# A graph layer with residual and normalisation: more pairs turned by VectorE, normalisation one pair later, a part of it on VectorE, loads issued from two queues

## The reference

```python
# x: 50000 x 512 float32; src, dst: 62500 edges, among them one loop per node; W_l, W_r: 512 x 512
msg  = x[src]
agg  = segment_sum(msg, dst, num_segments=n)
deg  = segment_sum(ones, dst, num_segments=n)
mean = agg / maximum(deg, 1.0)[:, None]
h    = mean @ W_l + b + x @ W_r
out  = layernorm(x + h * sigmoid(h), axis=-1)      # (u - mean(u)) / sqrt(var(u) + 1e-5)
```

## Time and profile before

| | |
|---|---|
| median of three executions | 1533.49 us (1531.86 to 1535.54) |
| the profiled execution | 1532.49 us, of which 1530.7 us are its span |
| PE busy | 1498.7 us (98% of the span) |
| PE weight loads | 1240.8 us (81%) |
| DVE busy | 1320.3 us (86%) |
| ACT busy | 1180.0 us (77%) |
| POOL busy | 1025.4 us (67%) |
| moved by DMA | 397.68 MB, mean 260 GB/s |

### The profile page before, as it was taken

The page is one execution under the profiler, slowest core; times in us unless marked ns, Lnnn a source line. Parts: engine busy times, 40 slices in busy tenths (PEclk is TensorE's granted clock), DMA queues, the critical chain, the costliest instruction groups (busy, mean ns, idle before and its releaser), DMA issues.

```text
span 1530.7 us, 23969 instructions
## 1 busy us (share of the span) xinstructions
PE 1498.7 (98%) x7198; PEld 1240.8 (81%) x7198; DVE 1320.3 (86%) x2090; ACT 1180.0 (77%) x1603; POOL 1025.4 (67%) x1089
## 2 busy tenths in 40 slices
PE   8999999999999999999999999999999999999996
PEld 6887778888888778888888888888888888888885
DVE  7988999999997878888888888888888888887886
ACT  5454333333334889999999999999999999999997
POOL 6446566666662766766767767667777777777774
PEclk9999999999999999999999999999999999999998
DMA  6476688989987789999989999999999999999996
GB/s 208 156 223 189 203 253 266 267 260 264 268 267 214 205 251 287 287 276 278 276 263 298 274 283 282 277 280 270 277 285 270 279 275 288 289 274 270 291 271 199
DMA packets 299349, 397.68 MB, mean 260 GB/s; under 512 B 43036, under 2 KB 145206, under 8 KB 299221
## 3 DMA queue, kind: packets, MB, share of 16 engines
q1 hardware_dynamic: 252277, 321.93, 70.5%
q0 software_dynamic: 46944, 74.22, 18.0%
HBM read 333.87 MB, written 139.67 MB: 309 GB/s over the span
## 4 chain that ended last, share of the span: by engine, by line
PE 68%; ACT 8%; issue 8%; DMA 5%; DVE 5%; POOL 5%; SPq 0%; POOLq 0%; ACTq 0%; DVEq 0%
PE pH L546 61%; DMA cor<-correction_rows,node_idx 4%; PE pT L651 3%; PE pT L620 3%; ACT cor L755 2%; ACT O L808 2%; POOL cor L452 2%; ACT pH L823 1%; ACT Z L835 1%; POOL rstd L516 1%; POOL var_eps L513 1%; PE pT L557 1%; POOL light_cor L452 1%; DVE Z L914 1%; DVE xs L1102 0%
## 5 line engine op out<-in xcount | busy, mean ns | idle before, releaser
L452 POOL DMA_INDIRECT cor<-correction_rows,node_idx x347 | 396.1, 1141 | 241.6 <-ACT cor L755 138.7
L546 PE MATMUL pH<-ws_hi,x_hi 128*128 128x512 f32 x876 | 347.3, 396 | 6.2 <-ACT pH L823 2.5
L546 PE MATMUL pH<-ws_hi,x_lo 128*128 128x512 f32 x876 | 343.3, 392 | 0.0
L546 PE MATMUL pH<-ws_lo,x_hi 128*128 128x512 f32 x876 | 342.3, 391 | 0.0
L546 PE MATMUL pH<-wb_hi,x_hi 128*128 128x512 f32 x688 | 275.5, 400 | 1.4 <-DVE x_lo L1090 1.3
L546 PE MATMUL pH<-wb_hi,x_lo 128*128 128x512 f32 x688 | 268.3, 390 | 0.0
L546 PE MATMUL pH<-wb_lo,x_hi 128*128 128x512 f32 x688 | 267.9, 389 | 0.0
L808 ACT ACTIVATE O<-Z,shift,rstd 128x512 f32<-128x512 f32 x347 | 262.7, 808 | 2.0 <-DVE shift L1137 1.9
L1127 DVE BATCH_NORM_STATS2 stats<-Z 128x6 f32<-128x512 f32 x347 | 219.4, 674 | 0.0
L729 ACT ACTIVATE s_hi<-sums 128x512 fp32r<-128x512 f32 x98 | 62.1, 634 | 196.8 <-issue 163.7
L1119 DVE TENSOR_TENSOR Z<-Z,X 128x1024 f32<-128x1024 f32 x174 | 211.3, 1214 | 1.1 <-ACT Z L835 1.1
(11 more groups left out here) (147 smaller groups left out, 2758.5 us busy)
## 6 DMA issues: line engine op xcount, KB each, us to landing
X<-in_x SPq DMA_DIRECT2D x173, 512.0 KB
out<-O SPq DMA_DIRECT2D x173, 512.0 KB
xs<-in_x SPq DMA_DIRECT2D x344, 128.0 KB
correction_rows<-c_out SPq DMA_DIRECT2D x98, 256.0 KB
light_x<-in_x SPq DMA_DIRECT2D x51, 256.0 KB, 2.9
light_h<-early_product SPq DMA_DIRECT2D x44, 256.0 KB
out<-light_o SPq DMA_DIRECT2D x44, 256.0 KB
join_row<-joined SPq DMA_DIRECT2D x98, 64.0 KB
```

Of the source, the lines that this page charges most:

```text
L452: g.indirect_dma_start(out=out_, out_offset=None, in_=table, in_offset=bass.IndirectOffsetOnAxis(ap=idx, axis=0), bounds_check=bound, oob_ ...
L546: last = mm(ps, a[:, k], w[:, k], start=(n == 0 and not onto), stop=(n == len(terms) - 1), skip_group_check=onto)
```

## The change

Pairs with t % 5 in (1, 2, 4) are turned by DVE, the others by PE. x_raw and x_blocks get a second buffer (in `xd`, which the edge tiles used before), each with a semaphore of its own. Of the four DMAs that load a pair's blocks, SP issues two and ACT two. ACT's two stand in its list between `seed` and `reset_cor`. DVE's `turn_blocks` moves from the end of its step to the place behind `residual`. `make_shift`, `normalise` and `store_out` come one pair later; mv, rstd and shift get four buffers, and the waits that guarded two are loosened. Pairs with t % 6 == 0 are normalised by DVE, as (Z - mean)·rstd in two instructions at the end of its step, and need no shift.

```diff
         def by_blocks(t):
-            return t % 2 == 1 and t < NP - 1
+            return t % 5 in (1, 2, 4) and t < NP - 1
...
+        def block_ring(t):
+            n = turned_by_dve(t) - 1
+            return n % 2, n // 2
+
+        def normed_by_dve(t):
+            return t % 6 == 0
...
             def load_blocks(t):                                        # SP
-                wait(sp, blocks_turned, (t + 1) // 2 - 1)
-                first = BASE + 2 * t * P
-                for j in range(4):
...
+                wait(sp, blocks_turned, turned_by_dve(t) - 2)
+                for j in range(2):
+                    sp.dma_start(*block_part(t, j)).then_inc(blocks_in[block_ring(t)[0]], 16)
...
             def move(t, q, u):
                 if by_blocks(t + 3):
                     load_blocks(t + 3)
                 shifted(t, q, u, 3, NP, load_x)
-                shifted(t, q, u, -3, NP, store_out)
+                shifted(t, q, u, -4, NP, store_out)
                 lights(light, t)
...
             def make_rstd(t, q, u):                                    # POOL
                 wait(pool, mv_made, 2 * t + 2)
-                wait(pool, shift_made, t - 1)
-                wait(pool, normed, t - 1)
+                wait(pool, normed, t - 3)
...
+            def load_blocks(t):                                        # ACT
+                wait(act, blocks_turned, turned_by_dve(t) - 2)
+                for j in range(2, 4):
+                    act.dma_start(*block_part(t, j)).then_inc(blocks_in[block_ring(t)[0]], 16)
+
             def normalise(t, q, u):                                    # ACT
+                if normed_by_dve(t):
+                    return
                 nt, rows = pair_shape(t)
                 b, used = ring(q, u, 2)
-                wait(act, shift_made, t + 1)
+                wait(act, shift_made, shifts(t))
                 wait(act, stored[b], 16 * used)
+                wait(act, normed, t)
...
             single(0, round_x)
+            act.wait_ge(diff_made, ET)
+            load_blocks(1)
+            load_blocks(2)
...
+                if by_blocks(t + 3):
+                    load_blocks(t + 3)
                 shifted(t, q, u, 3, NP, reset_cor)
                 lights(light, t)
-                shifted(t, q, u, -3, NP, normalise)
+                shifted(t, q, u, -4, NP, normalise)
             peeled(0, NP, node_pair)
+            single(NP - 4, normalise)
             single(NP - 3, normalise)
...
+            def normalise(t, q, u):                                    # DVE
+                if not normed_by_dve(t):
+                    return
+                nt, rows = pair_shape(t)
+                b, used = ring(q, u, 2)
+                wait(dve, stored[b], 16 * used)
+                wait(dve, rstd_made, t + 1)
+                wait(dve, normed, t)
+                for a in range(nt):
+                    last = v.tensor_scalar(O[0:rows, b, a], Z[0:rows, u % 4, a], mv[0:rows, u, a, 0:1],
+                                           rstd[0:rows, u, a:a + 1], ALU.subtract, ALU.mult)
+                last.then_inc(normed, 1)
...
                 shifted(t, q, u, -1, NP, residual)
-                shifted(t, q, u, -2, NP, make_shift)
-                lights(light, t)
                 if by_blocks(t + 2):
                     single(t + 2, turn_blocks)
+                shifted(t, q, u, -3, NP, make_shift)
+                lights(light, t)
+                shifted(t, q, u, -4, NP, normalise)
             peeled(0, NP, node_pair)
```

More of the change, by code:

```diff
@@ L34, in gnn_layer @@
     assert (NTILES - EARLY) % 2 == 1 and ET % 2 == 0 and NP % 2 == 0 and COLS <= 512
-    assert 4 * EARLY == NP + 2
+    assert 4 * EARLY == NP + 2 and all((NP - n) % 6 for n in range(1, 6))
     LATE = 28
@@ L78, in gnn_layer @@
         stats = sb("stats", [P, 2, 2, nc.vector.BN_STATS_DIM], f32)
[L79 to L82, removed]
+        mv = sb("mv", [P, 4, 2, 2], f32)
+        var_eps = sb("var_eps", [P, 4, 2], f32)
+        rstd = sb("rstd", [P, 4, 2], f32)
+        shift = sb("shift", [P, 4, 2], f32)
         node_idx = sb("node_idx", [P, NTILES + 1], i32)
@@ L93, in gnn_layer @@
         xs = sb("xs", [P, 4, D], f32)
-        x_raw, x_blocks = xs[:, 0:2], xs[:, 2:4]
-        xd = [sb(f"xd{b}", [P, D], f32) for b in range(4)]
+        xd = sb("xd", [P, 4, D], f32)
+        x_raw, x_blocks = (xs[:, 0:2], xd[:, 0:2]), (xs[:, 2:4], xd[:, 2:4])
         diff = sb("diff", [P, 2, D], f32)
@@ L177, in gnn_layer @@
         cor_in = [sem(f"cor_in{b}") for b in range(4)]
-        blocks_in, blocks_turned = sem("blocks_in"), sem("blocks_turned")
+        blocks_in, blocks_turned = [sem(f"blocks_in{b}") for b in range(2)], sem("blocks_turned")
         transposed, hi_made, lo_made, product, z_made, silu_made = (sem("transposed"), sem("hi_made"), sem("lo_made"),
@@ L207, in by_blocks, with turned_by_dve, shifts, block_part @@
         def by_blocks(t):
-            return t % 2 == 1 and t < NP - 1
+            return t % 5 in (1, 2, 4) and t < NP - 1
         def turned_by_pe(t):
-            return t // 2 + 1 + t // (NP - 1)
+            return sum(not by_blocks(p) for p in range(t + 1))
+        def turned_by_dve(t):
+            return sum(by_blocks(p) for p in range(t + 1))
+        def block_ring(t):
[3 more added lines that the diff above has]
+            return t % 6 == 0
+        def shifts(t):
+            return sum(not normed_by_dve(p) for p in range(t + 1))
+        def block_part(t, j):
+            first = BASE + 2 * t * P
+            return (x_raw[block_ring(t)[0]][32 * j:32 * j + 32].rearrange("r a (i c) -> r (a i) c", i=4),
+                    x[first:first + 2 * P, j * P:(j + 1) * P].rearrange("(i r) c -> r i c", r=32))
         def in_blocks(tile):
@@ L645, in transpose_x @@
                 pe.wait_ge(x_in[b], 16 * (used + 1))
-                if fixed(t) and t < 2:
-                    pe.wait_ge(sums_made, ET - 1 + t)
+                if fixed(t) and t < 4:
+                    pe.wait_ge(sums_made, min(ET - 1 + t, ET))
                 wait(pe, lo_made, t - 1)
@@ L792, in round_x @@
                 if by_blocks(t):
-                    act.wait_ge(blocks_turned, (t + 1) // 2)
-                    a_(in_blocks(x_hi[b]), x_blocks.rearrange("p a (i k r) -> p (a i) k r", k=K, r=32), ACT.Copy
+                    act.wait_ge(blocks_turned, turned_by_dve(t))
+                    a_(in_blocks(x_hi[b]), x_blocks[block_ring(t)[0]].rearrange("p a (i k r) -> p (a i) k r", k=K, r=32), ACT.Copy
                        ).then_inc(hi_made, 1)
@@ L1089, in split_x @@
                 if by_blocks(t):
-                    v.tensor_tensor(in_blocks(x_lo[b]), x_blocks.rearrange("p a (i k r) -> p (a i) k r", k=K, r=32),
+                    v.tensor_tensor(in_blocks(x_lo[b]), x_blocks[block_ring(t)[0]].rearrange("p a (i k r) -> p (a i) k r", k=K, r=32),
                                     in_blocks(x_hi[b]).bitcast(f32), ALU.subtract).then_inc(lo_made, 1)
@@ L1098, in turn_blocks @@
             def turn_blocks(t, q, u):
[L1099 to L1102, removed]
+                b, used = block_ring(t)
+                dve.wait_ge(blocks_in[b], 64 * (used + 1))
+                if used:
+                    held = [p for p in range(t) if by_blocks(p)][-2]
+                    dve.wait_ge(lo_made, held + 1)
+                v.transpose(x_blocks[b], x_raw[b]).then_inc(blocks_turned, 1)
             def add_cor(t, q, u):
@@ L1124, in moments @@
                 wait(dve, u_made, t + 1)
-                wait(dve, rstd_made, t - 1)
+                wait(dve, normed, t - 3)
                 for a in range(nt):
```

24 lines of the change are left out of this document (13 added, 11 removed).

## The result

The changed kernel takes 1563.86 us (median of 4 runs, 1562.27 to 1564.72). The kernel before took 1532.67 in the same series, so the ratio is 1.0205, interval 1.0193 to 1.0218: 31 us slower, where I had forecast 10 us faster. The profiled execution has a span of 1560.4 us.

What follows compares the result with a forecast made beforehand. PE was taken as the bound, before and after. From the profiled 1532.49 us, -15.7 (PE) +5 (PE's waits) +0.7 (the end) gave 1522.5, or 1523.5 as a median; own range 1517 to 1530, overall range 1515 to 1545.

Steps and rivals of the forecast that it cites:

- PE, -15.7 us: PE turns 70 pairs instead of 88; 18 x 0.87 = 15.7 us go, mean pair 5.80 us.
- everything covered: Rival: all other costs are covered and PE's own sum stands, 1533.5 - 15.7 = 1518 us; chance 0.06.
- POOL, SP, DMA, counted 0: POOL, SP's issues and loads, and 9.4 MB more on the DMA engines (5.95 us a pair) add no time.
- The second rival: DMA engines become the bound at 5.95 us a pair: 10 us slower, 1544 (1525 to 1570); chance 0.13.
- ACT, waits put on: Silu waits for the normalisation ahead: +0.09 us a pair for ACT's (16 us), +0.13 for DVE's (23 us).
- the third rival: Silu's two new waits eat the gain: 0.41 us a pair in place of 0.22 gives 1533, no change; chance 0.12.
- ACT's DMA issues, +0.1 us a pair of blocks: ACT's two issues between seed and reset_cor, about 1.35 us, mostly covered: 10 us, +0.06 a pair.
- The first rival: ACT becomes the bound through uncovered DMA issues before reset_cor: 27 us slower, 1561, or 1630 with all; chance 0.14.
- DVE +51 us: DVE gets 22 us of turns and 29 us of normalisations: 4.98 to 5.27 us a pair, 91%.
- Start 0: First 52 us of the stage: no change taken, between 2 us won and 4.4 us lost.
- Waits of PE, 5 us: PE sometimes waits because ACT, at 98% of PE's time, is uneven: 5 us, between 0 and 15.7.
- The sign to look for: The prediction is wrong if PE's busy time in the stage falls below 99%.

Runs made afterwards that it cites:

- e9: e4 with every fourth pair storing one row in place of its 256 (23 MB less); 1519.8 us, ratio 0.9926.
- e11: The kernel before, with every fourth pair storing one row in place of its 256; 1527.5 us, ratio 0.9973.
- e7: The kernel before, with SyncE issuing the four block DMAs in 17 further pairs into buffers nobody reads; 1546.0 us, ratio 1.0104.
- e4: Changed kernel without VectorE's normalisation, ScalarE's issues and the delay of one pair; pattern, second block buffers and early turn stay; 1553.7 us, ratio 1.0141.
- e6: e4 with block pairs read as plain rows of 2 KB: same bytes, a quarter of the packets, x scrambled; 1548.6 us, ratio 1.0139.
- e5: e4 with the old pattern (every second pair in blocks) put back; second block buffers and early turn stay; 1534.7 us, ratio 1.0038.
- e13: e9 with shift, normalisation and store one pair later; 1568.4 us, ratio 1.0238.
- e18: The whole changed kernel with a fifth buffer for Z, so silu overwrites the Z of t-5; 1550.2 us, ratio 1.0114.
- e1: Changed kernel with VectorE normalising no pair, ScalarE all of them; 1557.5 us, ratio 1.0164.
- e2: Changed kernel with all four DMAs of a block pair issued by SyncE, none by ScalarE; 1568.5 us, ratio 1.0234.
- e14: e9 with ScalarE issuing two of the four DMAs of each block pair; 1534.6 us, ratio 1.0001.
- e10: Changed kernel with every fourth pair storing one row in place of its 256; 1568.1 us, ratio 1.0239.

## Why the prediction was wrong, point by point

- *PE, -15.7 us: right for a steady pair, not for the whole.* In e9 a pair takes 5.81 us where I had 5.80, with PE full. Its 1519.8 us beside the 1518 of "everything covered" is in part luck, since 5 us of it are the stores (e11); against e11 the pattern is worth 7.7 us.
- *POOL, SP, DMA, counted 0: the step that failed.* I had worked out 5.95 us a pair for the DMA engines and then set it aside, "since the share is no cap: 12 us from 1181 show a share of 1.05 at 306 GB/s". This zero failed: twelve microseconds at 306 GB/s do not show that each load of the stage lands in time. The runs showed that the added block loads make DMAs late: loads alone cost 16 us with nobody reading them (e7), the pattern with its loads 22 us where -15.7 was forecast (e4), and waits for DMAs rise from 14 to 125 us there and to 47 in the changed kernel. As a rate, 1.643 MB a pair (279 x 5.89) become 1.697, which at PE's 5.80 us are the 293 GB/s that I asked for; e7 held 292 for 200 us with PE full. So a ceiling of the rate is not what failed, as far as these runs tell. The part to doubt is that SP's list "is not what ends last": the late loads stand behind the light tiles' in it. That this order is the cause is argued, not tried. The price by packets was the wrong question as well (e6).
- *The second rival was the main case.* I gave it 0.13 and 1544 us. Its sign was right, PE and DVE waiting for DMAs; its size (10 us) is half of what e4 shows (22 us, 1.4%, of which 0.4% come with the ring and the early turn, e5). The share stayed at 0.97, not above 1.0, and that the engines are full is not shown: e13 waits as long at 258 GB/s.
- *ACT, waits put on, 39 us of ACT's time with PE still the bound: the wait for DVE was mis-sized, and it cost time.* I took 0.8 us in 29 pairs; ACT stood idle 62.2 us in 29 pairs, 2.1 us each, so more than the upper end of 1.5. The two normalisations themselves were sized well (0.54 us each, 0.5 taken); DVE simply begins them late, behind light tile and turn. For the serial step I took 0.15 us in three quarters of the pairs; it stands in nearly all, 0.09 of gap and 0.10 of overlap. Together they cost the changed kernel 14 us (e18); VectorE's part taken out alone returns 6 (e1). As the third rival had it, this eats the gain; it comes on top of the late loads.
- *ACT's DMA issues, +0.1 us a pair of blocks: right for the changed kernel, not in general.* The two issues of a pair take 1.31 us (median of 104; 0.32 for the first and 0.96 for the second), near the 1.35 that I took from SyncE, and almost all of it is covered: reset_cor overlaps the seed by 0.05 us on average, 0.07 before. Undone, the kernel is no faster (e2). But on a kernel with PE full they cost 15 us (e14). The first rival, 27 us and more, did not come.
- *DVE +51 us: the place right, the size high.* Its busy time rose by 40 us (1320.3 to 1360.6), to 772.11/900 x 6.08 = 5.22 us a pair where 5.27 was forecast. *Start 0: right* (47.28 busy of 52, 47.59 before). *Waits of PE, 5 us: far too little*, by the terms above; PE stood idle 24 us in the window alone.
- *The sign to look for* was given: "wrong if PE's busy time in the stage falls below 99%". It fell to 97.4%.

A sum fitted afterwards: 1532.7, -15.7 for PE's transposes, about +37 for the rest of the pattern (e4's +22 over before, counted from PE's sum), +10 to 14 for silu's waits, 1564 to 1568; measured 1563.9. Its parts are e4 and e18. Taken alone they do not return as they were put on: with 23 MB of stores less the changed kernel gains nothing (e10).

## What to carry to other kernels

When the DMA engines are busy for nearly the whole stage, neither the share of busy time nor the mean rate tells what is left: here 54 KB more a pair cost time at 283 GB/s, while 292 GB/s went by with PE full. Ask for each load what stands ahead of it in its queue, sort the waits for it by the step that it belongs to, and see whether they fall on one step. A change that saves an engine's time by moving more bytes is worth testing with loads that nobody reads, added to the old kernel: that is one run, and it prices the loads alone. If bytes are then taken away as a test, note where in the queue they stood. And when a step is delayed by a pair, count the buffers: a ring of as many as the delay puts the last reader right in front of the next writer.

## What the runs showed of the hardware that was not expected

GpSimd's small operations took up to five times as long beside a VectorE operation with two operands from SBUF. In e5 the operations l_var_eps and l_rstd began together with the split of a block pair and the residual. Groups of POOL by line from 600 to 1500 us (count, busy us, mean ns), first of before, then of e5:

```profile
L495 POOL TENSOR_SCALAR l_var_eps<-l_mv 128x1 f32<-128x1 f32 x38 | 9.4, 247 | 1.2
```

```profile
L510 POOL TENSOR_SCALAR l_var_eps<-l_mv 128x1 f32<-128x1 f32 x38 | 34.2, 901 | 1.2
```

And one of them in e5's timelines, first POOL, then DVE:

```profile
899.59 1.23 POOL L510 TENSOR_SCALAR l_var_eps<-l_mv 128x1 f32<-128x1 f32 x1
900.90 1.40 POOL L512 TENSOR_TENSOR l_rstd<-l_var_eps,minus_half 128x1 f32<-128x1 f32 x1
```

```profile
899.54 1.19 DVE L1112 TENSOR_TENSOR x_lo<-xs,x_hi 128x1024 fp32r<-128x1024 f32 x1
900.65 1.22 DVE L1143 TENSOR_TENSOR Z<-Z,X 128x1024 f32<-128x1024 f32 x1
```

Each POOL operation ends just behind the DVE operation that it began beside (900.82 behind 900.73, 902.30 behind 901.87). Sorted by what DVE does as they begin, l_var_eps takes 1191 to 1231 ns beside x_lo<-xs,x_hi (26 times) and 242 to 247 beside the statistics (10 times); beside x_lo<-pT, whose first operand comes from PSUM, var_eps stays at 230 to 246 (49 times). The Trainium skill, SBUF — State Buffer, section SBUF: two separate sides, says that VectorE with two SBUF inputs and a GpSimd operation that reads SBUF exclude each other for a whole instruction; the trace agrees. A block pair's split has both operands in SBUF, a PE-turned pair's has not, so each further block pair holds GpSimd, behind whose small operations the next gather stands. How much of e4's and e5's loss that is, no run tells.
